# Two norms behind one square root, and the other experts' sort keys made inside the first search

## The chip, the cores and the metric

One core of a Trainium2 chip runs the whole kernel as one program. The number that counts is the device time of one execution in microseconds (us). The engines named here are TensorE (PE in the profile, with PEld for its weight loads), VectorE (DVE), ScalarE (ACT), GpSimd (POOL) and SyncE (SP, which only issues DMAs here). Each engine runs its own list of instructions in order, and they meet through semaphores.

## The reference

The input is x, 32 x 256 tokens of 128 features. Four layers follow each other: attention A, a feed-forward layer of eight experts, attention B, and the same feed-forward layer again.

```python
x = x + attn_a(_layernorm(x), ...)
x = x + ffn(_layernorm(x), ...)
x = x + attn_b(_layernorm(x), ...)
x = x + ffn(_layernorm(x), ...)

def ffn(x, centroids, ln_g, ln_b, w1, b1, w2, b2):
    norm = layer_norm(feat, ln_g, ln_b)            # a second norm, on the normed x
    scores = norm @ centroids.T                    # [8192, 8]
    sort_by_expert = balanced_assignment(scores)   # expert e takes the 1024 best of what is left
    routed = feat[sort_by_expert].reshape(E, C, D)
    h = gelu(layer_norm(routed, ln_g, ln_b) @ w1 + b1) @ w2 + b2
    # routed + h goes back to the tokens' places
```

So the feed-forward layer sees a norm of a norm. With the variance v of a token and eps = 1e-5, the first norm divides by sqrt(v + eps), and the second by the root of the normed token's own variance, v / (v + eps), plus eps.

## The kernel before, in words

The 8192 tokens are 64 tiles of 128 and stay in on-chip memory as `x`. The program is six phases, one after the other, with a barrier of all engines between them (L82, in `phase`): attention A, score stage, experts, attention B, score stage, experts. The score stage (`normalise_for_experts`) and the experts (`experts`) are thus run twice, with the same code. The change touches only these two phases and the helper `statistics`.

**The statistics.** Attention A and B leave in `halves` the counts, means and variances of the two halves of every token. `statistics` is a block of its own at the start of the score stage. DVE makes `var` (128 x 64, one number for each token, times 128) from them (L188 to L194). ACT takes its root (L214), DVE the reciprocal `rstd` and the product `shift` (L197, L198). DVE then scales `var` twice, ACT takes the second root, and DVE makes `rstd_2` and `shift_2`, the scale and offset of both norms together (L201 to L206). `Chain` makes each DVE step wait for the end of the one before.

**The scaling block.** It begins when all engines have left the statistics block and SP has raised ten semaphores (L758 to L761). In groups of four tiles DVE writes `norm` (L799), PE turns it by 128 x 128 (L834), ACT adds gain and bias (L870), PE multiplies by the centroids (L851), ACT copies the scores, PE turns them back (L841), and DVE puts them into `scores` (L806, called `place`). Four buffers `norm0` to `norm3` also go to memory as `norm_rows` (L766), and DVE fills a buffer again only when its store has landed. POOL first computes from both roots two numbers for each token that undo the scaling (`back`, L776 to L782) and adds them to each buffer (L788); SP's store of a group waits for that.

**The keys.** Behind the last group DVE turns all 128 x 512 scores into sortable integers of two 16-bit halves, `high_key` and `low_key` (L815 to L823).

**The search.** In `experts`, DVE first sets ten tables (L1052 to L1061). For each expert it then finds the 1024th best key among the tokens that are left, in eight passes: DVE compares all keys with 15 candidates (`reach`, L1183), PE counts (L1342), DVE waits for the count (L1193) and derives the next candidates (L1197 to L1205). Behind `reach` and ahead of the wait for the count stands a slot for other DVE work, `windows[n]`. It is filled from the second expert on (lists of the expert before, sums for the expert before that). In the first search the eight slots are empty. While no expert's matrices are being worked on, PE runs three extra matmuls behind each count (L1348), whose result nobody reads. The matrices themselves (L1255, L1268) begin two experts later.

## Time and profile before

| | |
|---|---|
| median of 3 runs | 1311.17 us (1309.95 to 1311.72) |
| the profiled execution | 1311.53 us, of which 1309.7 us are the span of the trace |
| mean granted TensorE clock | 0.95 |
| first score stage, from DVE's first instruction to its last | 525.83 to 559.03 us |
| first search, from `high_of` of expert 0 to that of expert 1 | 561.44 to 581.7 us |
| second score stage begins | 1023.03 us |

The busy shares on the page are means over six phases with different limits. For a change at the seams between phases the timeline around 526, 556 and 1023 us says more: it lists each instruction with its start, its length and, in brackets, how long its engine had been idle and what ended that. Where a row merges several like operations ("x20"), its length is that of the whole group and its bracket that of the first one. Windows give for a stretch the busy time of each engine and the granted clock (1.00 is 2.4 GHz, 0.50 is 1.2 GHz).

### The profile page before, as it was taken

To read this page: it belongs to the slowest core of one execution; us is meant where nothing else is said; L and a number is where in the kernel's file an instruction comes from. 1 tells how busy PE (TensorE), PEld (TensorE's weight loads), DVE (VectorE), ACT (ScalarE), POOL (GpSimd) and SP (SyncE) were. 2 spreads that over 40 slices of the span, in tenths; PEclk is the share of its full clock that TensorE was granted. 3 is DMA by queue.
4 is the path that set the end of the run, shared out by engine and by line. 5 is a ranking of instruction groups with operands and counts; after the bars stand their busy time and mean duration, and the time that the engine had idled before them with its cause. 6 is when DMAs were issued, how large, how long until landed. Compare 5 with 4: busy or idle time off the path is not lost. (4 is left out here: it accounts for less than half of the span.)

```text
span 1309.7 us, 34218 instructions
## 1 busy us (share of the span) xinstructions
PE 1139.3 (87%) x11708; PEld 733.5 (56%) x11708; DVE 877.4 (67%) x2747; ACT 674.9 (52%) x1452; POOL 776.7 (59%) x829
## 2 busy tenths in 40 slices
PE   4999999999999998667999994869999567999995
PEld 1444444444444444334777773759999334777774
DVE  6777767777777775778788711775655778878720
ACT  3777777677777765402434443575555411343353
POOL 2877888878778887102566674655555102456675
PEclk9999999999999999778999997889999787999998
DMA  8000000000000000410222222300000320122231
GB/s 195 3 1 0 0 0 0 0 0 0 0 0 0 0 1 2 145 33 20 56 65 78 61 71 80 76 1 1 0 0 0 105 75 19 52 56 65 60 87 38
DMA packets 55852, 47.33 MB, mean 36 GB/s; under 512 B 13142, under 2 KB 47190, under 8 KB 55772
## 3 DMA queue, kind: packets, MB, share of 16 engines
q1 hardware_dynamic: 44748, 27.92, 7.7%
q0 software_dynamic: 8192, 17.84, 4.8%
q10 hardware_dynamic: 2832, 0.54, 0.3%
q8 instruction: 46, 0.75, 0.2%
q14 instruction: 34, 0.28, 0.1%
HBM read 28.44 MB, written 17.83 MB: 35 GB/s over the span
## 5 line engine op out<-in xcount | busy, mean ns | idle before, releaser
L349 POOL TENSOR_TENSOR patt_aa<-patt_aa,causal_aa 128x512 f32<-128x512 f32 x256 | 319.4, 1275 | 73.1 <-DVE patt_aa L528 71.2
L528 DVE TENSOR_TENSOR patt_aa<-p_second_aa,first_aa 128x512 f32<-128x512 f32 x384 | 247.4, 686 | 134.3 <-ACT first_aa L424 130.8
L424 ACT ACTIVATE first_aa<-p_first_aa 128x512 f32<-128x512 f32 x384 | 208.4, 596 | 136.7 <-PE p_first_aa L627 132.8
L1430 POOL DMA_INDIRECT rows_e<-norm_rows,index_e x128 | 123.9, 968 | 196.2 <-DVE index_e L1119 161.4
L627 PE MATMUL p_second_aa<-q_t_aa,k_t_aa 32*128 32x512 f32 x768 | 235.0, 642 | 0.0
L627 PE MATMUL p_first_aa<-q_t_aa,k_t_aa 32*128 32x512 f32 x768 | 217.4, 642 | 15.0 <-ACT first_aa L424 14.7
L1255 PE MATMUL p_h_e<-rows_t_e,w_e 128*128 128x512 f32 x256 | 144.5, 674 | 13.8 <-ACT rows_t_e L1381 13.7
L646 PEld LDWEIGHTS p_z_aa<-patt_aa,v_aa 128*32 128x32 f32 x3072 | 72.2, 109 | 147.5 <-issue 78.9
L1391 ACT ACTIVATE hid_e<-p_h_e,b_e 128x512 f32<-128x512 f32 x128 | 88.5, 692 | 118.3 <-PE p_h_e L1255 118.3
L1268 PE MATMUL p_y_e<-w_e,hid_e 128*128 128x128 f32 x1024 | 131.1, 280 | 0.0
L646 PE MATMUL p_z_aa<-patt_aa,v_aa 128*32 128x128 f32 x3072 | 123.7, 279 | 2.8 <-POOL patt_aa L349 2.8
L1381 ACT ACTIVATE rows_t_e<-p_t_e,bias,gain 128x512 f32<-128x512 f32 x32 | 24.8, 776 | 194.3 <-PE p_t_e L1246 194.3
L1268 PEld LDWEIGHTS p_y_e<-w_e,hid_e 128*128 128x128 f32 x1024 | 119.7, 192 | 7.3 <-issue 7.3
L627 PEld LDWEIGHTS p_first_aa<-q_t_aa,k_t_aa 32*128 32x128 f32 x768 | 57.6, 183 | 96.5 <-ACT first_aa L424 87.1
L343 POOL TENSOR_TENSOR roped_aa<-straight_aa,crossed_aa 128x512 f32<-128x512 f32 x64 | 81.4, 1273 | 47.9 <-DVE crossed_aa L518 47.9
L1342 PE MATMUL p_cnt_e<-reach_e,ones_e 128*128 128x120 bf16 x896 | 75.6, 228 | 32.8 <-DVE reach_e L1183 32.5
L1342 PEld LDWEIGHTS p_cnt_e<-reach_e,ones_e 128*128 128x128 bf16 x896 | 56.5, 103 | 70.8 <-DVE reach_e L1183 48.0
L1255 PEld LDWEIGHTS p_h_e<-rows_t_e,w_e 128*128 128x128 f32 x256 | 72.0, 317 | 40.4 <-ACT rows_t_e L1381 20.5
L411 ACT ACTIVATE q_t_aa<-p_turn_aa,own_aa 128x512 f32<-128x512 f32 x128 | 81.5, 697 | 2.7 <-PE p_turn_aa L610 2.5
L1437 POOL DMA_INDIRECT out<-yb_e,index_e x64 | 65.0, 1016 | 23.4 <-issue 19.2
L1437 POOL DMA_INDIRECT ffn_rows<-yb_e,index_e x64 | 65.0, 1016 | 23.1 <-issue 19.2
L589 PE MATMUL p_turn_aa<-w_qk_aa,xn_t_aa 128*32 128x512 f32 x512 | 70.2, 621 | 7.9 <-DVE crossed_aa L518 6.5
(262 smaller groups left out, 2101.0 us busy)
## 6 DMA issues: line engine op xcount, KB each, us to landing
norm_rows<-norm_n SPq DMA_DIRECT2D x32, 288.0 KB, 2.7
w_e<-L_ffn_w SPq DMA_DIRECT2D x32, 256.0 KB, 2.9
x<-L_attn_a_x SPq DMA_DIRECT2D x8, 512.0 KB, 5.9
x<-ffn_rows SPq DMA_DIRECT2D x7, 512.0 KB, 7.0
rows_e<-norm_rows,index_e POOLq DMA_INDIRECT x128, 2.6
ffn_rows<-yb_e,index_e POOLq DMA_INDIRECT x64
out<-yb_e,index_e POOLq DMA_INDIRECT x64
x<-ffn_rows SPq DMA_DIRECT2D x2, 256.0 KB, 3.5
```

The source lines that it names most:

```text
L349: pool.tensor_tensor(patt[n % LAG][:, b, :, :], patt[n % LAG][:, b, :, :], causal[:, None, :].broadcast_to([P, 4, P]), ALU.mult).then_inc( ...
L411: act.activation(q_t[par][:, :, j, :], p_turn[:, :].rearrange("p (h q) -> p h q", h=HALVES), ACT.Identity, scale=own[:, j:j + 1]).then_inc ...
L424: act.activation(first[n % 2][:, b, :], p_first[b][:], ACT.Identity).then_inc(first_copied, 1)
L528: dve.tensor_tensor(patt[n % LAG][:, b, :, :].rearrange("p h q -> p (h q)"), p_second[(2 * n + b) % ROOMS][:], first[n % 2][:, b, :], ALU. ...
L627: pe.matmul(out[:], k_t[par][rows, half, keys * P:(keys + 1) * P], q_t[par][rows, half, :, queries * P:(queries + 1) * P], start=True, sto ...
L646: mm = pe.matmul(p_z[32 * c:32 * c + 32, queries * P:(queries + 1) * P], v[par][:, keys, 32 * h:32 * h + 32], patt[n % LAG][:, b, c, :], s ...
L1255: pe.matmul(p_h[m % 2][:], w1[par][:, f:F:FC], rows_t[:, h * 512:(h + 1) * 512], start=True, stop=True).then_inc(up_done, 1)
L1268: mm = pe.matmul(p_y[t // 4][:, (t % 4) * D:(t % 4 + 1) * D], hid[:, f, t * P:(t + 1) * P], w2[par][:, f, :], start=False, stop=(t % 4 == ...
L1342: mm = pe.matmul(p_cnt[:, 0:SPAN * CANDS], ones[:], reach[:, q // 4, :, (q % 4) * SPAN:(q % 4 + 1) * SPAN], start=(q == 0), stop=(q == TIL ...
L1391: act.activation(hid[:, f, h * 512:(h + 1) * 512], p_h[m % 2][:], ACT.Gelu_apprx_tanh, bias=b1[par][:, f:f + 1]).then_inc(gelu_done, 1)
L1430: pool.indirect_dma_start(rows[lpar][:, j, :], None, norm_rows, bass.IndirectOffsetOnAxis(ap=list_of(l, lpar)[:, j:j + 1], axis=0)).then_i ...
L1437: pool.indirect_dma_start(ffn_rows, bass.IndirectOffsetOnAxis(ap=list_of(c, par)[:, j:j + 1], axis=0), yb[par][:, j, :], None).then_inc(sc ...
```

## The change

1. The block `statistics` is gone. Its work stands at the head of DVE's part of the scaling block. The root of both norms together is taken in one step: sqrt(var * (1 + eps) / 128 + eps * eps), which is the product of the two roots. Its reciprocal is `rstd_2`. A second root `std_1`, for the first norm alone, is taken by ACT right behind it, and DVE makes `rstd` and `shift` of it (`first_scale`) behind the first group of four tiles. POOL's four steps for `back` wait for these.
2. ACT takes a root of two constants (`warm`) before it waits for `var`.
3. Only expert 0's keys (128 x 64) are made in the score stage. The other seven's (128 x 448) are made in the slots of the first search, and so are seven of the ten tables. PE waits for those seven (`set_late`) ahead of the ranking in search 0, and its extra matmuls read `lanes` instead of `sixteenth`.

```diff
-        statistics(nc, sem, k, tag, twice=True)
...
-                pool.tensor_scalar(moved[:], k["std_1"][:], 1.0, None, ALU.add).then_inc(back_step, 1)
+                pool.wait_ge(first_ready, 2)
+                pool.tensor_scalar(moved[:], k["rstd"][:], 1.0, None, ALU.add).then_inc(back_step, 1)
...
+                dve.memset(eps[:, 0:1], EPS).then_inc(var_done, 1)
+                dve.memset(eps[:, 1:2], EPS * EPS).then_inc(var_done, 1)
...
+                def first_scale():
+                    dve.wait_ge(std_done, 2)
+                    dve.reciprocal(k["rstd"][:], std_1[:]).then_inc(first_ready, 1)
+                    dve.wait_ge(first_ready, 1)
+                    dve.scalar_tensor_tensor(k["shift"][:], msum[:], -0.5, k["rstd"][:], ALU.mult, ALU.mult).then_inc(first_ready, 1)
...
+                    if g == 0:
+                        first_scale()
...
                 act.wait_ge(k["norm_consts"], 16 * 3)
+                act.wait_ge(var_done, 2)
+                act.activation(warm[:], eps[:], ACT.Sqrt).then_inc(warmed, 1)
+                act.wait_ge(var_done, 3)
+                act.activation(std_both[:], var[:], ACT.Sqrt, bias=eps[:, 1:2], scale=(1.0 + EPS) / D).then_inc(std_done, 1)
+                act.activation(std_1[:], var[:], ACT.Sqrt, bias=eps[:, 0:1], scale=1.0 / D).then_inc(std_done, 1)
...
-        SETUP = 10
+        SETUP = 3
+        LATE = 7
...
+                def sets_late():
+                    return [[lambda: late_link(dve.tensor_copy(table[:], digits[:, HALF:PASSES, :, None].broadcast_to([P, HALF, CANDS, WIDE])))],
+                            [lambda: key_link(dve.tensor_scalar(flip[:], others, 31, -2**31, ALU.arith_shift_right, ALU.bitwise_or)),
+                             lambda: late_link(dve.memset(ones_f[:], 1.0))],
+                            [lambda: key_link(dve.tensor_tensor(key[:], others, flip[:], ALU.bitwise_xor))],
+                            [lambda: key_link(dve.tensor_scalar(flip[:], key[:], 16, 0xffff, ALU.arith_shift_right, ALU.bitwise_and)),
+                             lambda: late_link(dve.tensor_scalar(minus_before[:], before[:], -1.0, None, ALU.mult))],
+                            [lambda: key_link(dve.tensor_copy(k["high_key"][:, 1:E, :], flip[:])),
+                             lambda: late_link(dve.tensor_scalar(sixteenth[:, 0:SLOTS, :], eighth[:, 0:SLOTS, :], float(LOW), None, ALU.mult))],
+                            [lambda: key_link(dve.tensor_scalar(flip[:], key[:], 0xffff, None, ALU.bitwise_and)),
+                             lambda: late_link(dve.tensor_scalar(sixteenth[:, SLOTS:HIGH, :], eighth[:, 0:SLOTS, :], float(LOW), float(LOW * SLOTS),
+                                                                 ALU.mult, ALU.add))],
+                            [lambda: key_link(dve.tensor_copy(k["low_key"][:, 1:E, :], flip[:]))],
+                            [lambda: fold_half(0), lambda: fold_half(1)]]
...
-                    windows = [[] for _ in range(PASSES)]
+                    windows = [[] for _ in range(PASSES)] if e else sets_late()
...
+                    if e == 0:
+                        pe.wait_ge(set_late, LATE)
```

DVE at the start of the score stage, behind the first memset, before (`gap_n` stands for `gap` and `gap2`, `rstd_n` for `rstd_2`):

```order
L189 TENSOR_TENSOR moment_n<-halves 128x64
L190 TENSOR_TENSOR gap_n<-halves 128x64
L191 TENSOR_TENSOR msum_n<-halves 128x64
L192 TENSOR_TENSOR gap_n<-gap_n 128x64
L194 SCALAR_TENSOR_TENSOR var_n<-gap_n,moment_n 128x64
L197 RECIPROCAL rstd<-std_n 128x64
L198 SCALAR_TENSOR_TENSOR shift<-msum_n,rstd 128x64
L201 TENSOR_TENSOR gap_n<-var_n,rstd 128x64
L202 TENSOR_TENSOR var_n<-gap_n,rstd 128x64
L204 RECIPROCAL gap_n<-std_n 128x64
L205 TENSOR_TENSOR rstd_n<-rstd,gap_n 128x64
L206 TENSOR_TENSOR shift_n<-shift,gap_n 128x64
```

And now:

```order
L759 MEMSET eps_n 128x1
L760 TENSOR_TENSOR gap_n<-halves 128x64
L761 TENSOR_TENSOR gap_n<-gap_n 128x64
L762 TENSOR_TENSOR moment_n<-halves 128x64
L764 SCALAR_TENSOR_TENSOR var_n<-gap_n,moment_n 128x64
L765 TENSOR_TENSOR msum_n<-halves 128x64
L768 RECIPROCAL rstd_n<-std_both_n 128x64
L769 SCALAR_TENSOR_TENSOR shift_n<-msum_n,rstd_n 128x64
L782 TENSOR_SCALAR norm_n<-x,rstd_n,shift_n 128x128 x4
L773 RECIPROCAL rstd<-std_n 128x64
L775 SCALAR_TENSOR_TENSOR shift<-msum_n,rstd 128x64
L782 TENSOR_SCALAR norm_n<-x,rstd_n,shift_n 128x128 x16
```

Between `var` and the first tile stood seven DVE operations; now there are three, `msum` among them. `rstd` and `shift` of the first norm stand behind the first four tiles.

DVE in the fifth pass of the first search (its first on the low half of the keys), before:

```order
L1183 TENSOR_TENSOR reach_e<-low_of_e,first_cand_e 128x480 x2
L1189 TENSOR_SCALAR level_e<-high_of_e,high_limit_e 128x64
L1193 TENSOR_REDUCE count_e<-p_cnt_e 128x15
L1197 SCALAR_TENSOR_TENSOR passed_e,base_e<-count_e,weight 128x15
L1201 TENSOR_SCALAR cand_e<-table_e,base_e 128x60
L1183 TENSOR_TENSOR reach_e<-low_of_e,cand_e 128x480 x2
L1193 TENSOR_REDUCE count_e<-p_cnt_e 128x15
```

And now:

```order
L1194 TENSOR_TENSOR reach_e<-low_of_e,first_cand_e 128x480 x2
L1200 TENSOR_SCALAR level_e<-high_of_e,high_limit_e 128x64
L1066 CAST high_key<-flip_e 128x448
L1067 TENSOR_SCALAR sixteenth_e<-eighth 128x512
L1204 TENSOR_REDUCE count_e<-p_cnt_e 128x15
L1208 SCALAR_TENSOR_TENSOR passed_e,base_e<-count_e,weight 128x15
L1212 TENSOR_SCALAR cand_e<-table_e,base_e 128x60
L1194 TENSOR_TENSOR reach_e<-low_of_e,cand_e 128x480 x2
L1068 TENSOR_SCALAR flip_e<-key_e 128x448
L1069 TENSOR_SCALAR sixteenth_e<-eighth 128x512
L1204 TENSOR_REDUCE count_e<-p_cnt_e 128x15
```

Two operations have come between each compare and the wait for its count (L1204 now), one of 448 columns for the other experts' keys and one of 512 for a table.

## Rows read from the trace of the kernel before

**Rows 1.** The page, part 1: busy time, share and instructions of each engine.
```profile
PE 1139.3 (87%) x11708; PEld 733.5 (56%) x11708; DVE 877.4 (67%) x2747; ACT 674.9 (52%) x1452; POOL 776.7 (59%) x829
```

**Rows 2.** Timeline, first score stage: start, length, engine, line, tiles, [idle, releaser].
```profile
525.83 0.06 DVE L188 MEMSET eps_n<- 128x1 f32 x1 [1.06 <-PEq L82]
...
527.10 0.22 DVE L194 SCALAR_TENSOR_TENSOR var_n<-gap_n,moment_n 128x64 f32<-128x64 f32 x1
527.42 0.35 ACT L214 ACTIVATE std_n<-var_n,eps_n 128x64 f32<-128x64 f32 x1 [4.36 <-DVE var_n L194]
527.80 0.55 DVE L197 RECIPROCAL rstd<-std_n 128x64 f32<-128x64 f32 x1 [0.48 <-ACT std_n L214]
...
531.57 0.38 POOL L776 TENSOR_SCALAR moved_n<-std_n 128x64 f32<-128x64 f32 x1
531.76 5.58 DVE L799 TENSOR_SCALAR norm_n<-x,rstd_n,shift_n 128x128 f32<-128x128 f32 x20 [1.14 <-SPq L761]
...
533.49 3.21 SPq L766 DMA_DIRECT2D norm_rows<-norm_n  x4
534.31 0.71 PEld L834 LDWEIGHTS p_t_n<-ident,norm_n 128*128 128x128 f32 x4 [0.29 <-DVE norm_n L799]
```

**Rows 3.** Timeline, second score stage, same columns.
```profile
1023.03 0.06 DVE L188 MEMSET eps_n<- 128x1 f32 x1 [1.20 <-PEq L82]
...
1024.61 1.28 ACT L214 ACT_TABLE_LOAD   x1 [4.58 <-DVE var_n L194]
1025.90 0.35 ACT L214 ACTIVATE std_n<-var_n,eps_n 128x64 f32<-128x64 f32 x1
...
1030.21 5.52 DVE L799 TENSOR_SCALAR norm_n<-x,rstd_n,shift_n 128x128 f32<-128x128 f32 x20 [1.12 <-SPq L761]
```

**Rows 4.** Timeline, first score stage, DVE ahead of its sixth group.
```profile
538.89 0.19 DVE L806 TENSOR_SCALAR scores<-p_sct_n 128x32 f32<-128x32 f32 x1 [1.55 <-PE p_sct_n L841]
```

**Rows 5.** The stores' line L766: who waited for it, time to landing.
```profile
  DVE norm_n L799: 0.3, 1
...
DMA to landing us min/median/max: 2.4/2.7/3.9
```

**Rows 6.** Timeline, end of first score stage and start of first search.
```profile
556.29 0.43 DVE L815 TENSOR_SCALAR flip_n<-scores 128x512 int32<-128x512 int32 x1
...
558.61 0.42 DVE L823 CAST low_key<-scores 128x512 uint16<-128x512 int32 x1
...
559.93 0.17 DVE L1052 MEMSET ones_e<- 128x128 bf16 x1 [0.90 <-PEq L82]
...
561.44 0.19 DVE L1175 TENSOR_TENSOR high_of_e<-high_key,avail_e 128x64 uint16<-128x64 uint16 x1
```

**Rows 7.** Groups by line and shape, DVE: busy, mean ns | idle before.
```profile
L1081 DVE TENSOR_SCALAR rounded_e<-slot_e 128x64 f32<-128x64 f32 x16 | 3.5, 218 | 0.6
...
L817 DVE TENSOR_TENSOR key_n<-scores,flip_n 128x512 int32<-128x512 int32 x2 | 1.4, 693 | 0.1
...
L1057 DVE TENSOR_SCALAR sixteenth_e<-eighth 128x512 bf16<-128x512 bf16 x2 | 0.6, 284 | 0.0
```

**Rows 8.** Timeline, first search: two of the eight waits for a count.
```profile
567.89 0.28 DVE L1193 TENSOR_REDUCE count_e<-p_cnt_e 128x15 f32<-128x120 f32 x1 [0.69 <-PE p_cnt_e L1342]
...
572.64 0.28 DVE L1193 TENSOR_REDUCE count_e<-p_cnt_e 128x15 f32<-128x120 f32 x1 [0.33 <-PE p_cnt_e L1342]
```

**Rows 9.** Waits of DVE within the first search: total, times, longest.
```profile
DVE count_e L1193 <- PE p_cnt_e L1342: 4.3, 8, 0.8
```

**Rows 10.** Stretches: length, busy of each engine, PE clock granted, DMA, GB/s.
```profile
556.00:558.00 2.00, 0.02 (x1) 0.00 (x0) 1.84 (x5) 0.00 (x0) 0.00 (x0) 1.00 0.00 0
558.00:562.20 4.20, 0.00 (x0) 0.01 (x1) 3.20 (x16) 0.00 (x0) 0.53 (x2) 0.50 0.02 1
562.20:568.10 5.90, 5.73 (x32) 3.10 (x33) 3.43 (x15) 0.00 (x0) 0.64 (x3) 0.50 0.11 13
...
632.00:640.00 8.00, 7.55 (x56) 6.45 (x54) 7.51 (x28) 2.26 (x4) 6.17 (x7) 1.00 0.20 54
```

More of the change, by code:

```diff
@@ L715, in ps @@
             return ctx.enter_context(nc.psum_tensor(f"{name}_{tag}", [P, 512], F32))
-        k = {**k, "rstd_2": sb("rstd_2", [P, TILES]), "shift_2": sb("shift_2", [P, TILES]),
-             "std_1": sb("std_1", [P, TILES]), "std_2": sb("std_2", [P, TILES])}
-        statistics(nc, sem, k, tag, twice=True)
+        k = {**k, "rstd_2": sb("rstd_2", [P, TILES]), "shift_2": sb("shift_2", [P, TILES])}
+        halves = k["halves"]
+        moment = sb("moment", [P, TILES])
+        gap = sb("gap", [P, TILES])
+        gap2 = sb("gap2", [P, TILES])
+        msum = sb("msum", [P, TILES])
+        var = sb("var", [P, TILES])
+        std_1 = sb("std_1", [P, TILES])
+        std_both = sb("std_both", [P, TILES])
+        eps = sb("eps", [P, 2])
+        warm = sb("warm", [P, 2])
+        stat_step = sem(f"stat_step_{tag}")
+        var_done = sem(f"var_done_{tag}")
+        std_done = sem(f"std_done_{tag}")
+        warmed = sem(f"root_warmed_{tag}")
+        first_ready = sem(f"first_scale_ready_{tag}")
         norm = [sb(f"norm{i}", [P, GROUP, WIDTH]) for i in range(NB)]
@@ L726, in normalise_for_experts @@
         p_sct = [ps(f"p_sct{i}") for i in range(NB)]
-        flip = sb("flip", [P, E, TILES], I32)
-        key = sb("key", [P, E, TILES], I32)
+        flip = sb("flip", [P, 1, TILES], I32)
+        key = sb("key", [P, 1, TILES], I32)
+        low = sb("low", [P, 1, TILES], I32)
         p_t = [ps(f"p_t{i}") for i in range(2)]
@@ L793, in _ @@
             def _(dve):
+                link = Chain(dve, stat_step)
+                dve.memset(eps[:, 0:1], EPS).then_inc(var_done, 1)
+                dve.memset(eps[:, 1:2], EPS * EPS).then_inc(var_done, 1)
+                link(dve.tensor_tensor(gap[:], halves[:, :, 1], halves[:, :, 4], ALU.subtract))
+                link(dve.tensor_tensor(gap2[:], gap[:], gap[:], ALU.mult))
+                link(dve.tensor_tensor(moment[:], halves[:, :, 2], halves[:, :, 5], ALU.add))
+                dve.scalar_tensor_tensor(var[:], gap2[:], D / 4.0, moment[:], ALU.mult, ALU.add).then_inc(var_done, 1)
+                link(dve.tensor_tensor(msum[:], halves[:, :, 1], halves[:, :, 4], ALU.add))
+                dve.wait_ge(std_done, 1)
+                link(dve.reciprocal(k["rstd_2"][:], std_both[:]))
+                link(dve.scalar_tensor_tensor(k["shift_2"][:], msum[:], -0.5, k["rstd_2"][:], ALU.mult, ALU.mult))
+                def first_scale():
[3 more added lines that the diff above has]
+                    dve.scalar_tensor_tensor(k["shift"][:], msum[:], -0.5, k["rstd"][:], ALU.mult, ALU.mult).then_inc(first_ready, 1)
                 def turn(g, b, i):
@@ L944, in experts @@
         tok_hi = sb("tok_hi", [P, SLOTS])
+        flip = sb("flip", [P, E - 1, TILES], I32)
+        key = sb("key", [P, E - 1, TILES], I32)
         index = [sb(f"index{i}", [P, SLOTS], U32) for i in range(4)]
@@ L996, in experts @@
         wait_passed = sem(f"passed_{tag}")
+        keyed = sem(f"keyed_{tag}")
+        set_late = sem(f"set_late_{tag}")
         def plan(eng, turn):
@@ L1058, in _, with fold_half @@
-                dve.tensor_scalar(sixteenth[:, SLOTS:HIGH, :], eighth[:, 0:SLOTS, :], float(LOW), float(LOW * SLOTS), ALU.mult, ALU.add).then_inc(sv, 1)
-                dve.tensor_scalar(minus_before[:], before[:], -1.0, None, ALU.mult).then_inc(sv, 1)
-                for half in range(2):
+                late_link = Chain(dve, set_late)
+                key_link = Chain(dve, keyed)
+                others = k["scores"][:, 1:E, :].bitcast(I32)
+                def fold_half(half):
                     dve.tensor_reduce(fold[:, half, :, :], k["ident"][:].rearrange("p (c k h s) -> p h k s c", c=4, k=2, h=2)[:, half, :, :, :],
-                                      AX.X, ALU.add).then_inc(sv, 1)
+                                      AX.X, ALU.add).then_inc(set_late, 1)
```

60 lines of the change are left out of this document (8 added, 52 removed).

## The prediction, as it was put on record

> **What bounds the kernel now.** I read the page first: PE is busy 87% of the span, DVE 67% [rows 1]. That says where not to look: the change takes almost nothing from PE. So the question is whether it touches a stretch in which PE stands still and everybody waits for DVE. The timeline shows two such stretches in each of the two feed-forward layers. The first is the head of the score stage: DVE starts at 525.83, and the first tile is scaled at 531.76 [rows 2]. In these 5.93 us only one operation at a time runs, on DVE or ACT. In the second layer it is 1023.03 to 1030.21, or 7.18 us, with a table load of 1.28 us in it [rows 3]. The other stretch is the seam to the experts: six key operations from 556.29 to 559.03 (the last starts at 558.61 and takes 0.42), 0.90 us of barrier, and ten tables until the first search begins at 561.44 [rows 6]. From 556.0 to 562.2 PE has 0.02 us of work [rows 10]. Every microsecond removed in these seams moves all that follows, as the phases are separated by barriers. What matters is what comes late instead.
>
> **Part 1, one root and no block of its own.** Before, the first memset to the end of `var` takes 527.10 + 0.22 - 525.83 = 1.49 us [rows 2]. One operation of about 0.27 with its 0.03 of chain (`msum`) goes behind `var`, where ACT's root hides it, and a short memset is added (0.03): 1.22. ACT starts 0.10 after `var` ends (527.32 to 527.42) and takes 0.35; the reciprocal starts 0.03 later and takes 0.55 [rows 2]; the product is a 128x64 operation of about 0.22 [rows 7], with 0.03 of chain on either side. First tile at 1.22 + 0.10 + 0.35 + 0.03 + 0.55 + 0.03 + 0.22 + 0.03 = 2.53 us against 5.93: **3.40 us less**. The barrier and SP's semaphores, whose end released the first tile before [rows 2], are then met early, beside the statistics.
>
> In the second layer the table load can start after the two memsets, at about 0.2, and ends at 1.48. The root of two constants costs between nothing and the 0.35 of a 128x64 root; as it has almost no columns, I take 0.20. The real root starts at 1.68 instead of 1.32, the first tile at 2.89 against 7.18: **4.29 us less**. If the load stayed behind `var`, 0.9 of it would be lost.
>
> The Trainium skill ("ScalarE: Activation LUTs", section "What ACT_TABLE_LOAD costs") gives about 1.28 us for the load and another 1.38 for a drain at every switch. The trace agrees with the first and not with the second: the load at 1024.61 takes 1.28, and the root starts at 1025.90, right at its end [rows 3]. By the page the root would start at 3.06 and the forecast below would be 1.4 us later; the sum goes by the row.
>
> **What comes late instead.** `first_scale` stands on DVE between the first and second group, and the second group waits behind it: 0.55 + 0.03 + 0.22 + 0.04 = 0.84 us. Before, PE took the second group 534.31 - 531.76 = 2.55 after the first tile, and was released by DVE [rows 2]. Twenty tiles take 5.58, so four take 1.12 [rows 2]; now it comes after 1.12 + 0.84 + 1.12 + 0.05 = 3.13, and 0.25 more if POOL's steps slow DVE as they do now on the first group (PE's 2.55 is 0.26 more than two groups and 0.05). The delay is 0.58 to 0.84; I take 0.75. From there on PE, ACT and DVE go round in turn, so this delay stays. **Score stage: 3.40 - 0.75 = 2.65 and 4.29 - 0.75 = 3.54, together 6.2 us.**
>
> The stores move less. POOL's chain begins now at 2.53 + 1.12 + 0.84 = 4.49, and the first store leaves 533.49 - 531.57 = 1.92 later, at 6.41 or 532.24, only 1.25 earlier than before [rows 2]. It lands 2.7 us later [rows 5], at 534.94. DVE comes to the fifth group, which needs that buffer, at 525.83 + 2.53 + 16 x 0.279 + 0.84 = 533.66 and waits 1.3 us; it ends it at 536.06. But after its fifth group DVE sits 1.55 us until PE releases it at 538.89 [rows 4]; 2.65 earlier is 536.24. So the late store is just covered, with 0.2 to spare; at nothing.
>
> **Part 2, keys.** Six operations over 512 columns take 2.74 us, of which the exclusive-or takes 0.69 [rows 6, 7]. Over 64 columns a single-input operation takes about 0.22 [rows 7], and I put the exclusive-or at 0.25; with the overlaps of the pairs as now, 0.25 + 0.28 + 0.13 + 0.25 + 0.13 + 0.22 = 1.26. Saved: 1.5 us. What hides behind them now is the last store; a store lands in 2.7 us, at most 3.9 [rows 5], and leaves before the last five scores are placed. If it were uncovered, it would cost some tenths.
>
> **Part 3, tables.** Ten tables take 559.93 to 561.44, or 1.51 us [rows 6]; three are left, two short ones and one of 60 columns, about 0.45. Saved: 1.06 us.
>
> **Part 4, the same work in the first search.** DVE waits for a count eight times, 4.3 us in total, 0.8 at most [rows 9]. The third wait is 0.69 and the fifth 0.33 [rows 8]; the first three lie in the stretch at clock 0.50 [rows 10] and are the long ones, 0.8, 0.76 (what lies between) and 0.69, so the last five share 4.3 - 2.25 = 2.05. What is put in: a copy (0.25); then 0.43 of shift plus a memset with chain 0.20; then the exclusive-or over 448 columns, 0.69 x 7/8 + 0.03 = 0.63. These three fit. The last five slots get 0.43 + 0.22, 0.43 + 0.31 (the 0.284 table [rows 7]), 0.43 + 0.32, 0.43 and 0.42: 2.99 us on 2.05 of waits. So 0.95 us stand out. Bounds: nothing, if they overlap better, and all 4.07 + 0.42 = 4.5 us, if nothing is covered. I take **0.95**, since the waits are the rows for the very same places. PE's new wait for `set_late` is met before the last pass ends.
>
> **Sum.** 6.2 + 2 x (1.5 + 1.06 - 0.95) = 6.2 + 3.2 = 9.4 us. The profiled execution took 1311.5 us and lies 0.36 above the median: 1311.53 - 9.4 = 1302.1, and against the median about **1301.8 us**. A measurement of this kernel tells 0.2% (2.6 us) from nothing; below 1308.5 is faster.
>
> **Rival A: the stores set the pace.** If the stage followed its stores and not DVE's first tile, it would gain 1.25 in the first layer. In the second the first store would leave at 2.89 + 1.96 + 1.92 = 6.77 against 7.18 + 1.73 = 8.91, 2.1 earlier. That is 3.4 instead of 6.2: 1304.6 us. For it: POOL's steps now stand behind `first_scale`, and the cover is 0.2 us. Against it: DVE waited for a store only once in both layers, 0.3 us [rows 5].
>
> **Rival B: the clock stays up.** PE's pause at the seam shrinks from 6.2 to 6.2 - 2.56 = 3.6 us. In it the granted clock went from 1.00 to 0.50 at about 558, and came back only at 568.1 [rows 10]. Were it kept, the first three waits would shrink from 0.76 to about 0.41, and of what DVE then has there some 0.45 would stand out: 1.05 - 0.45 = 0.6 a layer, 1300.6 us. Against it: before, it fell 2 us after PE stopped, and 3.6 is more.
>
> **Rival C: the moved work is not covered.** Then 4.5 us a layer come back where 2.56 were saved: 6.2 - 3.9 = 2.3 us of gain, 1308.9 us, no change that can be measured. It needs DVE to be the bound in the first search; 4.3 us of waits speak against it.
>
> **Rival D, on the other side: a full-clock stretch of the experts at half clock.** From 632 to 640 PE works 7.55 of 8 us at 1.00 [rows 10]. At 0.50 the same work takes 7.5 us more. The first search is where PE's pauses get longer, by the 0.95 us; if the granted clock fell there and stayed down into 10 us or more of such work, over both layers, the 9.4 would be gone. With 8 us lost to it in each layer the time is 1302 + 15 = 1317 us. It decides from 13 us of such work (12 us lost). For it: the clock does fall when PE pauses [rows 10]. Against it: the searches had pauses before, and the stretches behind them run at 1.00.
>
> **How the numbers follow.** The forecast 0.65 (its own range 1300 to 1303.5), A 0.14, B 0.10, C 0.06, D 0.05. Range 1299.3 to 1306: C and D lie outside. Faster: forecast, A, B and a little of C, 0.91; same 0.05; slower 0.04. That the two roots don't replace each other as said is no rival: the reciprocal of the joint root is what DVE now multiplies with.
>
> **What would show it.** First tile 2.5 us after the block's first memset in the first layer and 2.9 in the second, with the table load beside the statistics; PE's second group 3.1 to 3.4 after it; a wait of DVE for a store of about 1.3 before the fifth group; 1.3 us of keys and under 0.5 of tables; the first search longer by about 1 us, with DVE's waits gone in its last five passes; everything behind that only shifted. I am wrong if DVE's sixth group begins later than 536.5, if the search grows by more than 2 us, or if the experts' part is not the same length.

## The result and the profile after

The changed kernel took 1301.09 us at the median (1300.5 to 1304.17, four runs) against 1311.45 us (four runs); the ratio is 0.9929, with a 95% interval from 0.9914 to 0.9943. The forecast was 1301.8 us, from 1299.3 to 1306.0, and faster with 0.91. Six later runs of the same kernel gave 1302.82 us and a ratio of 0.9937 (0.9924 to 0.9949). The middle of all ten is 1302.6 us. Both intervals lie wholly below 1, so the change is faster, by 0.6 to 0.7%.

The profiled execution took 1300.5 us (span 1298.7), 11.0 us less than that of before. Where these are is best read off the places where a phase or a search begins, in two traces of each kernel (the second ones come from the repeats of both kernels that close the list of experiments). In us; pairs are the two traces, or the ends over traces and layers:

| | before | after | change, mean | forecast |
|---|---|---|---|---|
| score stage, layer 1: first memset to last scores | 30.4, 30.9 | 28.6, 28.2 | -2.2 | -2.65 |
| score stage, layer 2 | 31.7, 31.8 | 28.2, 28.2 | -3.55 | -3.54 |
| keys, each layer | 2.78 | 1.16 | -1.62 | -1.5 |
| barrier to the experts | 0.90 | 0.90 to 1.07 | +0.05 | 0 |
| tables | 1.51 | 0.34 | -1.17 | -1.06 |
| first search | 20.07 to 20.24 | 21.35 to 21.56 | +1.28 | +0.95 |
| third search, layer 1 | 25.94, 25.83 | 25.25, 25.98 | see the repeats | 0 |
| third search, layer 2 | 25.81, 25.49 | 24.87, 24.85 | see the repeats | 0 |

As the mean of both pairs, the edited stretches give 2.2 + 3.55 + 2 x (1.62 - 0.05 + 1.17 - 1.28) = 8.7 us, where 9.4 were forecast. In the first pair alone they give 8.3; the rest of its 11.0 us is not in the edited stretches: 1.6 us in the third searches, 0.5 and 0.3 us in attention A and B, and 0.3 in the later part of layer 1's experts.

The head of the first score stage, from the timeline of the changed kernel; these rows answer to [rows 2, 4]:

```profile
525.30 0.06 DVE L758 MEMSET eps_n<- 128x1 f32 x1 [1.07 <-PEq L82]
525.33 0.27 DVE L760 TENSOR_TENSOR gap_n<-halves 128x64 f32<-128x64 f32 x1
525.33 0.06 DVE L759 MEMSET eps_n<- 128x1 f32 x1
...
526.20 0.23 DVE L764 SCALAR_TENSOR_TENSOR var_n<-gap_n,moment_n 128x64 f32<-128x64 f32 x1
...
526.46 0.35 ACT L855 ACTIVATE std_both_n<-var_n,eps_n 128x64 f32<-128x64 f32 x1 [0.77 <-DVE var_n L764]
...
526.92 0.55 DVE L768 RECIPROCAL rstd_n<-std_both_n 128x64 f32<-128x64 f32 x1 [0.31 <-ACT std_both_n L855]
...
527.77 1.11 DVE L782 TENSOR_SCALAR norm_n<-x,rstd_n,shift_n 128x128 f32<-128x128 f32 x4
528.80 0.55 DVE L773 RECIPROCAL rstd<-std_n 128x64 f32<-128x64 f32 x1
...
529.69 0.51 POOL L739 TENSOR_SCALAR moved_n<-rstd 128x64 f32<-128x64 f32 x1 [4.06 <-DVE shift L775]
...
530.74 0.72 PEld L820 LDWEIGHTS p_t_n<-ident,norm_n 128*128 128x128 f32 x4 [1.08 <-DVE norm_n L782]
...
531.75 12.16 SPq L728 DMA_DIRECT2D norm_rows<-norm_n  x11
...
534.24 1.11 DVE L782 TENSOR_SCALAR norm_n<-x,rstd_n,shift_n 128x128 f32<-128x128 f32 x4 [1.21 <-DMA norm_rows<-norm_n]
...
536.03 0.19 DVE L791 TENSOR_SCALAR scores<-p_sct_n 128x32 f32<-128x32 f32 x1 [0.68 <-PE p_sct_n L827]
```

`var` ends 1.13 us after the first memset, ACT starts 0.03 later, and the first tile follows 2.47 us after the memset (5.93 before; 2.53 forecast). `first_scale` stands at 528.80. PE turns the second group at 530.74, 2.97 after the first tile (2.55 before). The first store leaves at 531.75, and DVE waits 1.21 us for it before the fifth group, at 534.24. The sixth group starts behind the first `place` (DVE's copy of a group's scores, which waits for PE) at 536.03, after 0.68 us of waiting.

PE's fourth group and the step that releases that `place`, first before and then in the changed kernel:

```profile
537.57 0.66 PE L834 MATMUL p_t_n<-ident,norm_n 128*128 128x128 f32 x4
...
538.52 0.33 PE L841 MATMUL p_sct_n<-ident,sc_t_n 128*128 128x128 f32 x1
```

```profile
534.01 1.11 PE L820 MATMUL p_t_n<-ident,norm_n 128*128 128x128 f32 x4
...
535.64 0.35 PE L827 MATMUL p_sct_n<-ident,sc_t_n 128*128 128x128 f32 x1
```

Counted from the first tile, the fourth group starts at 5.81 before and at 6.24 now. It takes 0.66 us before and 1.11 now, and the releasing step comes at 6.76 before and at 7.87 now.

The second layer, ACT and then DVE, which answer to [rows 3]:

```profile
1018.08 1.28 ACT L853 ACT_TABLE_LOAD   x1 [3.17 <-DVE eps_n L759]
1019.38 0.20 ACT L853 ACTIVATE warm_n<-eps_n 128x2 f32<-128x2 f32 x1
1019.49 0.33 ACT L855 ACTIVATE std_both_n<-var_n,eps_n 128x64 f32<-128x64 f32 x1
```

```profile
1017.91 0.06 DVE L758 MEMSET eps_n<- 128x1 f32 x1 [1.20 <-PEq L82]
...
1020.78 1.11 DVE L782 TENSOR_SCALAR norm_n<-x,rstd_n,shift_n 128x128 f32<-128x128 f32 x4
```

The load now runs from 1018.08, beside the statistics, and the real root starts 0.11 after the root of two constants has started. First tile after 2.87 us (7.18 before; 2.89 forecast).

The seam and four places in the first search, DVE, which answer to [rows 6, 8]; then DVE's wait for the count in the whole first search, which answers to [rows 9]:

```profile
553.93 0.20 DVE L801 TENSOR_SCALAR flip_n<-scores 128x64 int32<-128x64 int32 x1
...
554.86 0.19 DVE L809 CAST low_key<-low_n 128x64 uint16<-128x64 int32 x1
555.97 0.17 DVE L1048 MEMSET ones_e<- 128x128 bf16 x1 [0.91 <-PEq L82]
...
556.31 0.19 DVE L1186 TENSOR_TENSOR high_of_e<-high_key,avail_e 128x64 uint16<-128x64 uint16 x1
...
565.23 0.28 DVE L1204 TENSOR_REDUCE count_e<-p_cnt_e 128x15 f32<-128x120 f32 x1
...
568.22 0.28 DVE L1204 TENSOR_REDUCE count_e<-p_cnt_e 128x15 f32<-128x120 f32 x1
...
572.96 0.28 DVE L1204 TENSOR_REDUCE count_e<-p_cnt_e 128x15 f32<-128x120 f32 x1 [0.46 <-PE p_cnt_e L1353]
...
577.87 0.19 DVE L1186 TENSOR_TENSOR high_of_e<-high_key,avail_e 128x64 uint16<-128x64 uint16 x1
```

```profile
DVE count_e L1204 <- PE p_cnt_e L1353: 1.6, 4, 0.7
```

At 565.23 and 568.22 there is no wait left in brackets: DVE comes late to the count, as the slot ahead of it was fuller than the wait. Of 4.3 us of waits in eight places 1.6 us are left, in four: 0.70, 0.27 and 0.22 in the first three passes and the 0.46 at 572.96.

### The profile page after: what moved, and what is told of

It is laid out like the page before. It is cut to its first block and busy times, and to the rows that moved or that the text cites. A ratio compares the mean times of both kernels' runs of the same rounds, so it can differ in the third digit from the quotient of the medians.

```text
span 1298.7 us, 34222 instructions
## 1 busy us (share of the span) xinstructions
PE 1139.7 (88%) x11708; PEld 733.6 (56%) x11708; DVE 877.0 (68%) x2755; ACT 675.1 (52%) x1454; POOL 777.3 (60%) x829
## 5 line engine op out<-in xcount | busy, mean ns | idle before, releaser
L1394 ACT ACTIVATE rows_t_e<-p_t_e,bias,gain 128x512 f32<-128x512 f32 x32 | 24.8, 776 | 191.4 <-PE p_t_e L1257 191.4
```

## The experiments

Each time is the median of the runs named, each ratio is to the kernel before on the same chip. The whole kernel moves by up to 3 us either way from run to run. In the traces that lies mostly in attention A and B (the first score stage began at 525.3 to 527.3 us, and the stretch from the end of layer 1's experts to the second score stage took 208.9 to 213.4 us). So a difference of 1 us is read from the lengths of the edited stretches in the traces, not from the medians. There is one trace for each edit, so a single stretch rests on two values, one of each layer. The theories A, B and C of the first two expectations are not the prediction's rivals of the same letters: theory B is the prediction's rival A.

**Statistics alone.** The changed kernel with keys, tables and search slots as before.

```diff
-                mine = scores[:, 0:1, :].bitcast(I32)
-                dve.tensor_scalar(flip[:], mine, 31, -2**31, ALU.arith_shift_right, ALU.bitwise_or).then_inc(kept, 1)
+                dve.tensor_scalar(flip[:], scores[:].bitcast(I32), 31, -2**31, ALU.arith_shift_right, ALU.bitwise_or).then_inc(kept, 1)
...
-        SETUP = 3
-        LATE = 7
+        SETUP = 10
...
-                    windows = [[] for _ in range(PASSES)] if e else sets_late()
+                    windows = [[] for _ in range(PASSES)]
```

> The root in one step and the early table load alone; keys and tables stay as before. Theory A (the gain is made at the seams and adds up part by part): the traces give 1.8 us for the first score stage and 3.5 for the second, so 5.3 us less than before, about 1306. Theory B (the store of the first buffer paces the stage): 3.4 us less, about 1308. Theory C (part of the gain of the whole change is the place of the half-clock stretch in the third search, which moves with the seams): the third search shortens here by 0.3 to 0.9 us a layer as well, which A does not expect; then up to 7 us less.

Measured: 1304.15 us, ratio 0.9946 (0.9930 to 0.9961). The score stages took 28.55 and 27.91 us, 1.9 and 3.8 less than before; keys, tables and first search are as before (2.79, 1.51, 19.96 and 20.25). That is the 5.3 us of theory A within 0.4; the median says 6.4, the ratio's interval 5.1 to 9.2. Theory B's 3.4 us are out. On theory C: the third searches took 25.04 and 25.97, one shorter than before and one not.

**Keys and tables alone.** The kernel before with the new seam and slots.

```diff
...
-                    windows = [[] for _ in range(PASSES)]
+                    windows = [[] for _ in range(PASSES)] if e else sets_late()
```

> Keys of the other experts and seven tables inside the first search; statistics as before. Theory A: 2.8 us saved at the seam and 1.2 to 1.3 given back in the first search, in each layer, so 3.0 us less than before, about 1308.3. Theory B says nothing on it. Theory C: the third search shortens by 0.7 to 0.9 us here too, as the first search has the same length and pauses as in the changed kernel; then 4.6 us less.

Measured: 1307.02 us, ratio 0.9970 (0.9957 to 0.9983), 2.2 to 5.6 us less. Score stages 30.6 and 31.8, as before; keys 1.16 and tables 0.34; first search 21.58 and 21.38. So theory A's seam is there. The third searches took 26.02 and 24.85, again one of each kind. Theory C asked for both to shorten, and that did not happen.

**No early root.**

```diff
-                act.wait_ge(var_done, 2)
-                act.activation(warm[:], eps[:], ACT.Sqrt).then_inc(warmed, 1)
```

> The changed kernel without the root of two constants, so that the table load stands behind var again. Forecast's step: the first tile of the second layer comes 0.9 us later, 1302.0 against 1301.1; the first layer, which has no load, gains nothing or 0.1. Rival: the load costs the load and a drain, so 2.3 us later.

Measured: 1303.74 us, ratio 0.9942 (0.9924 to 0.9959), not to be told apart from the changed kernel by time. In the trace the first tile of the second layer comes 3.81 us after the memset instead of 2.87, the 0.9 expected, and that of the first layer 2.53 instead of 2.47. No drain appears: the rival's 2.3 us are out. The second layer's stage grew by more than the 0.9, though. It took 29.8 us where the changed kernel's took 28.2. The granted clock came back 7.9 us after the first tile instead of 6.5, and the first `place` came 8.25 us after it instead of 7.64.

**First norm's numbers one group later.**

```diff
-                    if g == 0:
+                    if g == 1:
                         first_scale()
```

> The first norm's reciprocal and product stand behind the second group of tiles instead of the first. Theory of the round trip (PE's second group waits for DVE, and this delay stays): PE's second group comes 0.4 to 0.8 us earlier after the first tile, in both layers, so up to 1.3 us less than the changed kernel. Theory of the stores: POOL's chain begins 1.1 us later, the first store lands 1.1 us later, DVE waits 1.1 us longer before its fifth group, and the stage ends 0.5 to 1 us later.

Measured: 1304.66 us, ratio 0.9951 (0.9934 to 0.9968). The score stages took 29.7 and 30.0 us, 1.3 and 1.8 longer than the changed kernel's. The waits of DVE in the first one:

```profile
DVE norm_n L782 <- DMA norm_rows<-norm_n: 2.2, 1, 2.2
```

The theory of the round trip had its first step right: PE's second group comes 2.20 us after the first tile instead of 2.98. It gained nothing by it, since DVE waits 2.2 us for the first store instead of 1.2, as the theory of the stores has it. The stage grew by more than that theory's 0.5 to 1 us. PE now stands still for 1.94 us ahead of its fifth group (535.83 to 537.77), and the granted clock falls again in the stage, in both layers. The row is of the first layer:

```profile
537.80:541.00 3.20, 3.20 (x25) 2.02 (x25) 2.12 (x10) 1.28 (x3) 0.68 (x4) 0.50 0.99 295
```

So of the two places tried `first_scale` stands at the better one in the changed kernel. There the store is covered with 0.68 us to spare (the wait of `place` at 536.03), where the prediction had 0.2.

**The slots dealt out by their waits.**

```diff
-                             lambda: late_link(dve.memset(ones_f[:], 1.0))],
-                            [lambda: key_link(dve.tensor_tensor(key[:], others, flip[:], ALU.bitwise_xor))],
+                            [lambda: key_link(dve.tensor_tensor(key[:], others, flip[:], ALU.bitwise_xor)),
+                             lambda: late_link(dve.tensor_scalar(sixteenth[:, 0:SLOTS, :], eighth[:, 0:SLOTS, :], float(LOW), None, ALU.mult))],
...
```

The eight slots now hold: table and first shift; exclusive-or and first `sixteenth`; second shift, `minus_before` and `ones_f`; cast; mask; cast; second `sixteenth`; both folds.

> The changed kernel with the moved work dealt out by the waits that were there: the shift of the keys joins the copy in the first slot, the exclusive-or and a table stand in the second, and slots four to six hold one cast or mask each. Forecast's step (what stands out of the waits is what the first search grows by): the five last slots hold 2.0 us on 2.05 of waits, so the first search takes 20.3 to 20.6 us instead of 21.4 to 21.6, and the kernel 2 us less than the changed one. Rival (the search grows by the number of chained steps, wherever they stand): it stays at 21.4.

Measured: 1301.95 us, ratio 0.9932 (0.9918 to 0.9945). The first search took 20.85 and 20.86 us, 0.6 less than the changed kernel's, not 1.1. The rival (the number of steps counts) is out; the forecast length, 20.3 to 20.6, was 0.3 us too good. In time, 2 us less were expected than for the changed kernel, and no gain can be told: 0.9932 against that kernel's 0.9929 and 0.9937. Part of the gain in the search is not on DVE. In the changed kernel the granted clock falls in the seventh pass (windows: start, length, busy PE, PEld, DVE, ACT, POOL, granted clock, DMA share, GB/s):

```profile
568.00:570.00 2.00, 0.99 (x9) 0.39 (x8) 1.86 (x8) 0.00 (x0) 0.00 (x0) 0.97 0.00 0
570.00:573.00 3.00, 2.83 (x16) 1.44 (x15) 2.29 (x11) 0.00 (x0) 0.00 (x0) 0.50 0.00 0
```

With the slots spread there is no fall in the same passes (0.97 is the mean of a stretch whose end has the next fall, at 577.3):

```profile
567.00:571.00 4.00, 2.43 (x21) 1.28 (x22) 3.45 (x15) 0.00 (x0) 0.00 (x0) 1.00 0.05 13
571.00:577.70 6.70, 3.57 (x32) 1.88 (x30) 5.43 (x27) 0.00 (x0) 0.00 (x0) 0.97 0.00 0
```

What that fall costs is told by another trace. The kernel of the last experiment but one has the same first search, slots included, and its clock differs only in that it does not fall in these passes of the first layer (window, and DVE's wait in the seventh pass):

```profile
569.50:576.00 6.50, 4.21 (x37) 2.11 (x38) 5.69 (x27) 0.00 (x0) 0.00 (x0) 1.00 0.00 0
```

```profile
572.51 0.28 DVE L1204 TENSOR_REDUCE count_e<-p_cnt_e 128x15 f32<-128x120 f32 x1 [0.17 <-PE p_cnt_e L1353]
```

That search took 21.21 us against 21.56 in the first trace of the changed kernel, and DVE waits 0.17 in the seventh pass instead of 0.46. So the fall is worth 0.35 us, and the full slots alone 21.21 - 20.23 = 0.98 us. The full slots seem to bring the fall on: it came in 15 of the 16 first searches with them, in 1 of 6 with empty slots, and in neither of the two of this kernel. But the one with empty slots (the second layer of the statistics-only kernel), and the second layers of the two kernels below that join the spread slots with extra matmuls, show that it can come without them.

**PE busy at the head of the stage.**

```diff
+                pe.wait_ge(k["consts"], 16 * 6)
+                for _ in range(8):
+                    pe.matmul(p_sct[NB - 1][:], k["before"][:], k["lanes"][:, 0:64, :].rearrange("p a n -> p (a n)"), start=True, stop=True)
                 turn_rows(0, 0)
```

> The changed kernel with eight extra matmuls of 512 columns on PE at the head of each score stage, while DVE makes the statistics; their result is not read. If the half clock of the first round trips sets the head of the stage, the clock is back at 1.00 before or at PE's second group, and DVE's sixth group begins 1 to 2 us earlier. If the first store sets it, the fifth group still begins when the store lands, 6.5 us after the first tile, and the stage shortens by 0.7 us at most.

Measured: 1302.89 us, ratio 0.9942 (0.9927 to 0.9958). Windows of it in the first layer, same columns:

```profile
529.70:532.00 2.30, 2.30 (x7) 0.87 (x5) 2.23 (x9) 0.00 (x0) 0.33 (x1) 0.50 0.00 0
532.00:537.00 5.00, 3.33 (x38) 1.87 (x37) 3.79 (x15) 3.62 (x7) 1.93 (x9) 0.97 0.46 137
```

The clock is at 1.00 from 532.3, which is 2.6 us after the first tile and ahead of PE's second group, as expected. In the changed kernel it has 0.50 up to 535.7, 8.0 us after the first tile, and in the kernel before up to 537.5, or 5.8 us after it (the first row is of the changed kernel, the other two of the kernel before):

```profile
532.50:535.40 2.90, 2.90 (x24) 1.72 (x24) 1.65 (x7) 1.52 (x5) 0.32 (x2) 0.50 0.94 276
```

```profile
533.30:536.50 3.20, 3.17 (x19) 2.19 (x20) 3.20 (x14) 1.72 (x3) 0.68 (x5) 0.50 0.64 191
537.00:540.00 3.00, 2.90 (x35) 1.59 (x34) 1.45 (x7) 2.57 (x5) 0.64 (x3) 0.91 0.81 238
```

From first tile to first `place` it is 7.50 us here against 8.26 and 8.39 in the changed kernel and 7.13 before, and the stage takes 27.3 us against 28.6 and 28.2. In the second layer the first `place` came after 7.49 instead of 7.64, and the stage takes 28.4, no less. DVE's sixth group came 0.8 to 0.9 us earlier in the first layer, not 1 to 2. The fifth group still begins 6.5 us after the first tile, when the store has landed, as the theory of the store has it; but the first layer's stage shortened by 0.9 to 1.3 us, more than that theory's 0.7. So neither theory holds alone: the half clock accounts for the first layer's shortfall against the forecast, and the store puts a limit to what can be won by the clock.

**PE busy at the seam.**

```diff
+                for _ in range(6):
+                    pe.matmul(p_t[0][:], k["before"][:], k["lanes"][:, 0:64, :].rearrange("p a n -> p (a n)"), start=True, stop=True)
...
+                for _ in range(3):
+                    pe.matmul(p_h[0][:], before[:], lanes[:, 0:LOW, :].rearrange("p a n -> p (a n)"), start=True, stop=True)
```

Six stand on PE at the end of the score stage, three at the start of the experts.

> The changed kernel with six extra matmuls on PE at the end of the score stage and three at the start of the experts, so that PE pauses for about 1 us at a time at the seam instead of 3.4 us. Rival B of the prediction, made to happen: the granted clock stays 1.00 into the first search, whose first three waits shrink by 0.35, 0.27 and 0.22, so 0.8 us less in each layer. If the clock falls all the same, nothing changes.

Measured: 1303.47 us, ratio 0.9943 (0.9927 to 0.9960): no gain in time that can be told. Windows in the first search:

```profile
556.10:560.00 3.90, 2.71 (x24) 1.30 (x22) 3.27 (x13) 0.00 (x0) 0.98 (x5) 1.00 0.06 6
560.00:566.00 6.00, 2.95 (x23) 1.28 (x22) 5.51 (x25) 0.00 (x0) 0.00 (x0) 1.00 0.60 167
571.00:577.10 6.10, 4.44 (x30) 2.54 (x28) 4.45 (x23) 0.00 (x0) 0.00 (x0) 0.74 0.00 0
```

The clock does stay at 1.00 into the search. The first three waits shrink from 0.70, 0.27 and 0.22 us to 0.36, 0.03 and 0.03, the 0.8 us expected. The search shrinks to 21.04 and 20.98 us, by 0.5 rather than 0.8: the clock falls later in it, as it also did in the changed kernel, and this time the last pass waits 0.34 us too.

**Slots and both groups of matmuls.** The three edits above together.

> All three together. If each acts at its own place: the first search takes no more than 20.6 us, the score stage 0.5 us less than the changed kernel's, so 2.5 to 3.5 us less in all. If slots and clock share one cover (at full clock the first three waits are shorter, and the work that the spread slots put there stands out), the two give together no more than the better of them.

Measured: 1299.20 us, ratio 0.9910 (0.9895 to 0.9925). First search 20.62 and 20.89; score stages 27.7 and 28.5. In the first search they are better than the spread slots alone by 0.2 us in one layer and by nothing in the other. With the spread slots the full clock has only 0.25 us to take from the first three waits (0.28, 0.04 and 0.04 us, and now 0.03 or 0.04 each), where it took 0.8 with the slots of the changed kernel: slots and clock do share their cover. The stage gains 0.5 to 0.9 us in the first layer. By the ratios the time lies 2.5 to 3.5 us under the changed kernel's, as the other theory had it, but the stretches that the three edits touch do not add up to that: they are 1.9 us shorter than the mean of the changed kernel's two traces. Both third searches were of the short kind in it (24.85, 24.89), so a part of the gain is not its own.

**Before once more.** No edit.

> The kernel before, unchanged, for a second trace. If the third search's length (25.8 to 25.9 us in the first trace, 24.8 to 26.1 over the traces so far) is a property of the kernel, it repeats to 0.1 us; if it depends on where the half-clock stretch happens to fall in an execution, it can differ, and so can the length of attention A and B. The seams (5.93 and 7.18 us to the first tile, first search 20.24) repeat to 0.3 us in either case.

Measured: 1310.05 us. The seams repeat: 5.93 and 7.19 us to the first tile, first search 20.23 and 20.07. The third searches took 25.83 and 25.49. The stretch with attention B took 208.9 us where it had taken 211.7.

**Changed kernel once more.** No edit.

> The changed kernel, unchanged, for a second trace and more times. If the 1.6 us of the third searches belong to the change, both are again 24.9 to 25.3 and the time is 10.3 us under the kernel before. If they are luck of one execution, at least one is near 26.0 in this trace, and the median lies 8.5 to 10.5 us under before, with the seams' 8.3 us the part that stays.

Measured: 1302.82 us, ratio 0.9937 (0.9924 to 0.9949), 8.3 us under before (6.7 to 10.0). The third searches took 25.98 and 24.85. The cause of the third search's spread is visible in the two first traces. The first row is of the kernel before, the others of the changed one (windows, same columns):

```profile
608.00:612.40 4.40, 4.25 (x13) 2.08 (x13) 4.26 (x14) 2.75 (x3) 2.04 (x2) 0.50 0.19 50
```

```profile
604.60:607.20 2.60, 2.60 (x11) 1.51 (x10) 2.46 (x9) 1.86 (x2) 1.66 (x2) 0.50 0.24 57
607.20:611.00 3.80, 3.80 (x22) 2.57 (x21) 3.69 (x14) 2.06 (x3) 0.00 (x0) 0.97 0.07 19
```

And the first expert's matmuls before, on PE:

```profile
609.01 3.78 PE L1255 MATMUL p_h_e<-rows_t_e,w_e 128*128 128x512 f32 x4
```

Before, they fell almost wholly into the half clock, which ended at 612.6; four took 3.78 us. In the changed kernel the fall came some 1.4 us earlier after the search's start, and the clock was back at 607.4, in the midst of the same matmuls (from 605.2).

Twelve traces, with the two kernels and every mixture, have the same work on PE between search 1 and search 2. In each of their 24 third searches the clock is at 0.50 for one stretch of 6.8 us. The search's length follows the place of that stretch: where it ends 6.0 to 6.3 us after the search's start, the search took 24.76 to 24.96 us; at 6.5 to 6.9, 25.0 to 25.3; at 7.5, 25.5 and 25.6; at 8.1 to 8.6, 25.8 to 26.1. The place differs between two executions of one program: in the first layer of the changed kernel it ended at 6.8 in one trace and at 8.35 in the other. Whether the change also moves its mean is not shown. The four searches of the kernel before took 25.5 to 25.9 us, 25.8 at the mean; the twenty others took 24.8 to 26.1, 25.4 at the mean.

**PE busy around the third search.**

```diff
+                    if e == 1:
+                        for _ in range(3):
+                            pe.matmul(p_h[0][:], ones[:], lanes[:, 0:LOW, :].rearrange("p a n -> p (a n)"), start=True, stop=True)
...
+                        if e == 2 and n == 0:
+                            for _ in range(4):
...
```

Nobody reads these: three ahead of search 1's last pieces, two behind its `rank_chosen`, and four behind the first count of search 2.

> The changed kernel with nine extra matmuls on PE in each layer: three and two in the pauses around the ranking of search 1, four behind the first count of search 2. If PE's pauses there let the clock fall, it now stays at 1.00 or falls later and for less, and the third search takes under 24.9 us in both layers. If the fall has another cause, it takes 24.8 to 26.1 as before.

Measured: 1299.20 us (1298.24 to 1299.5), ratio 0.9910 (0.9897 to 0.9923). The third searches took 24.74 and 24.59 us, and the clock does not fall in them at all, in either layer (windows, first layer):

```profile
600.25:604.25 4.00, 2.88 (x24) 1.36 (x20) 3.69 (x15) 0.72 (x1) 3.09 (x4) 1.00 0.26 60
604.25:608.25 4.00, 3.68 (x22) 2.42 (x20) 3.86 (x13) 2.72 (x4) 1.63 (x2) 1.00 0.22 51
```

PE's timeline shows what differs: its pause ahead of the list of the chosen, 0.96 us before, is down to 0.30, and that ahead of the first expert's rows, 0.9 to 1.2 us before, to 0.29. Pauses of up to 0.6 us are left. The first expert's matmuls (604.59) run at full clock, four in 2.06 us:

```profile
598.94 0.81 PE L1375 MATMUL p_h_e<-lanes,ones_e 128*128 128x512 bf16 x3
...
600.94 0.70 PE L1353 MATMUL p_cnt_e<-reach_e,ones_e 128*128 128x120 bf16 x8 [0.20 <-DVE reach_e L1194]
601.48 1.03 PE L1362 MATMUL p_h_e<-lanes,ones_e 128*128 128x512 bf16 x4
602.80 0.63 PE L1257 MATMUL p_t_e<-ident,rows_e 128*128 128x128 f32 x4 [0.29 <-DMA rows_e<-norm_rows,index_e]
...
604.59 2.06 PE L1266 MATMUL p_h_e<-rows_t_e,w_e 128*128 128x512 f32 x4
```

The five runs lie within 1.3 us, and 3.6 us under the changed kernel on the same chip (interval of the ratios 0.9897 to 0.9923 against 0.9924 to 0.9949). Of the 3.6 the third searches of the two traces account for 1.5 (25.98 + 24.85 against 24.74 + 24.59). The two traces differ by 5.0 us in all, and 4.2 of these lie in the stretches with attention A (525.42 against 526.89 us up to the first score stage) and attention B (209.5 against 212.2), which the edit does not touch. So only the 1.5 us are shown to be the edit's; whether the rest of the medians' 3.6 is, stays open.

**All of it together.** Spread slots, matmuls at head, seam and third search.

> Spread slots, extra matmuls at head, seam and third search together. If each acts at its own place: 1 to 3 us less than the changed kernel with spread slots and the first two groups of extra matmuls, 1296 to 1298. If the clock's fall is only moved from one place to another, no less than that kernel.

Measured: 1298.89 us, ratio 0.9911 (0.9897 to 0.9925). Third searches 24.72 and 24.60, first searches 20.62 and 21.47, score stages 28.0 and 28.9. That is 0.9 us above the 1296 to 1298 of the first theory, and it is not faster than the third-search edit alone: in its second layer neither first search nor stage gained anything. In that search the clock, kept up at the seam, fell 7.9 us in and stayed at 0.50 for 6.8 us, so there the fall was only moved.

## Why the prediction was right

**The head of the stage: right.** 2.47 and 2.87 us to the first tile for 2.53 and 2.89; the statistics-only kernel and the one without the early root show both parts at their places and sizes, 0.9 us for the early load, and no drain.

**What comes late instead: right in kind, too small in the first layer.** The delay of PE's second group was 0.42 us (2.97 - 2.55), less than the 0.75 I took. DVE was not slowed as feared, and its operations overlapped by some 0.2 us around `first_scale`, which the sum of 3.13 laid end to end. But the first `place` came 1.15 us later than before, counted from the first tile. The term that was missing is the clock: before, it was back at 1.00 in time for PE's fourth group, 5.8 us after the first tile. Now PE pauses for 0.68 us behind its first group, for `first_scale`, and worked at 0.50 until 8.0 us after the first tile: the fourth group brought 0.7 of the 1.15 us, the pause 0.4. Two kernels bear this out. With PE busy at the head, the first `place` came 0.8 us sooner. With `first_scale` one group later, and so without the pause, the clock was back after 5.2 us in the first layer (6.4 in the second). Counted from the first memset, as the forecast's times were, DVE's sixth group began at 10.84 us, past the 10.67 (536.5) that the prediction had set as a sign of being wrong; on the clock of the trace it is 536.14 only because the whole stage began 0.5 us earlier.

In the second layer the clock was back after 6.5 us, early in the fourth group, which took 0.75 us, and the forecast held (3.55 for 3.54). That is not a property of the layer. In the seam and third-search kernels, whose heads are the same, it was back after 8.8 and 9.4 us in the second layer; their first `place` came after 8.39 us instead of 7.64, and their stages took 28.8 and 29.2 us. So the hit on this term is in part luck: two errors of opposite sign, and a clock that came back at the earlier of its places in both traces.

**The late store: right.** 1.21 us of waiting for 1.3; the fifth group ended at 534.24 + 1.11 = 535.35, ahead of 536.03. One group later it is no longer covered, as that experiment showed. What I did not see: in the first trace a later store held DVE once more (0.4 us).

**Keys and tables: right,** 1.62 and 1.17 for 1.5 and 1.06.

**The first search: right in kind, 1.28 for 0.95.** Where the clock did not fall inside the search it grew by 0.98 us, which is the forecast's term. The rest, up to 0.35 us, came in the seventh and eighth pass from a fall of the clock inside the search. I had taken the clock only as a rival at the seam (B). There it did fall in all four searches of the changed kernel, between 2.0 us ahead of the search and its start, where it had fallen 3.4 to 4.3 us ahead; it came back 4.9 to 6.7 us into the search, where it had been 5.9 to 6.8.

**The rivals.** These are the prediction's letters. A is out: the two stages gained 5.8 us and not 3.4, though a store one group later does set the stage. C is out, with 1.28 us standing out and not 4.5. B did not happen of itself; made to happen it gave 0.5 us a layer and no measurable time. D's loss did not happen, but its subject, a half-clock stretch over the experts' matmuls, was real: where it lies against the first expert's matmuls is worth up to 1.3 us a layer. It fell out in favour of the change in three of four searches. The place differs from execution to execution of one kernel, so one trace says nothing on what an edit does to it. By the prediction's last sign of being wrong, that the experts' part keeps its length, this was a miss: behind the first search it was 1.0 and 0.9 us shorter in the two layers of the first pair, most of it in the third searches.

So the 1301.8 us came out near 1301.1 partly by luck: the edited stretches gave 0.7 us less than forecast, and the first four runs lay 1.5 us under the middle of all ten.

What stays open: what shifts the clock's fall and return between two executions of one kernel, whether the full slots bring on the fall inside the first search, and whether the 2.1 us of the third-search edit that its own stretch does not show are the edit's.

## What to carry to other kernels

At a seam where every engine waits for one chain, count the chain operation by operation; it came out to 0.1 us. Work that is moved into waits should be dealt out by the length of each wait, and the sum over all slots is not enough. After such an edit ask what the clock of TensorE does in the longer pauses it makes: it was the one term missing here, at the head of the stage and in the search. A few matmuls that nobody reads, in the pauses ahead of heavy matmuls, gave 1.5 us in their own stretch and 3.6 us at the medians, where the whole rewrite gave 8.3 on the same chip. The same at two other places gave nothing that could be told. And take more than one trace of a kernel before a difference of 1 us in a stretch with heavy matmuls is put down to an edit.

## What the runs showed of the hardware that was not expected

- A table load of 1.28 us followed by a root that starts 0.01 to 0.02 us after it, with no drain, in both kernels.
- One search took 24.76 to 26.10 us over twelve traces with the same work on PE in it, by where a stretch of 6.8 us at 1.2 GHz lies against its matmuls; two executions of one program differed by 0.7 us in it (25.25 and 25.98). With PE's pauses ahead of the heavy matmuls cut from 0.9 to 1.2 us to 0.3, the clock stayed at 2.4 GHz in that search, in both layers of both kernels that had this.
- Two writes of one column to the same tile and the first subtraction started within 0.03 us of each other (525.30 to 525.33).
